# Scores transposed at the source, in 512-query groups with a per-key bias and the softmax sum from a matmul, for the 17 heads with the flattest ALiBi slopes

## What is computed

```python
xn = _layernorm(x, axis=-1)
q = (xn @ Wq).reshape(b, s, 32, 128)
k, v = (xn @ Wkv)[..., :128], (xn @ Wkv)[..., 128:]
scores = jnp.einsum('bqhd,bkd->bhqk', q, k) * scale
scores = jnp.where(causal, scores + slopes[h] * (pos_k - pos_q), -jnp.inf)
attn = jax.nn.softmax(scores, axis=-1)
x = x + jnp.einsum('bhqk,bkd->bqhd', attn, v).reshape(b, s, h) @ Wo + ffn(xn)
```

## Time and profile before

| | us |
|---|---|
| median of 2 runs, slowest core | 5608.9 (5591.86 and 5625.94) |
| the profiled execution, slowest core | 5518.5 |
| its span, first to last instruction | 5516.9 |
| spans of the 8 cores in it | 5493.5 to 5516.9 |
| mean granted TensorE clock of the cores | 0.765 to 0.768 of 2.4 GHz |

### The profile page before, as it was taken

The page is one execution under the profiler, slowest core; times in us unless marked ns, Lnnn a source line. Parts: engine busy times, 40 slices in busy tenths (PEclk is TensorE's granted clock), DMA queues, the critical chain, the costliest instruction groups (busy, mean ns, idle before and its releaser), DMA issues.

```text
span 5516.9 us, 49355 instructions; the slowest of 8 cores (5493.5 to 5516.9 us)
## 1 busy us (share of the span) xinstructions
PE 3486.3 (63%) x16923; PEld 1724.7 (31%) x17216; DVE 1495.5 (27%) x3505; ACT 1086.5 (20%) x1984; POOL 165.7 (3%) x171
## 2 busy tenths in 40 slices
PE   1575565656634499964766665665655444548999
PEld 1332222222222244432322232333333222224444
DVE  4212222222234300023122223333333444442000
ACT  4001111111133300012011222222222333331000
POOL 0000000000000000000000000000000000000000
PEclk9887777777755599976887777767767666668999
DMA  5342322232151157733422312112114000002764
GB/s 120 59 68 47 55 47 42 37 55 47 32 101 41 37 111 150 147 107 92 61 48 46 55 32 42 29 32 39 32 32 77 17 25 17 17 17 63 151 137 100
DMA packets 293247, 340.03 MB, mean 62 GB/s; under 512 B 28688, under 2 KB 249872, under 8 KB 282640
## 3 DMA queue, kind: packets, MB, share of 16 engines
q0 software_dynamic: 244480, 163.75, 22.1%
q1 hardware_dynamic: 30096, 139.54, 7.6%
q10 hardware_dynamic: 18432, 33.56, 1.6%
HBM read 467.01 MB, written 33.55 MB: 91 GB/s over the span
## 4 chain that ended last, share of the span: by engine, by line
PE 54%; DVE 15%; issue 13%; ACT 9%; DMA 8%; DVEq 1%; ACTq 0%; POOL 0%; SPq 0%; POOLq 0%
PE ps_a L424 19%; PE ps_a L686 16%; DVE scratch L603 8%; PE ps_c L557 7%; ACT astream L613 6%; DMA wstream<-wq 4%; PE ps_t L522 4%; PE ps_s L596 3%; DMA scratch<-x 2%; DVE scratch L531 2%; PE ps_a L691 2%; DVE cols L619 1%; ACT scratch L534 1%; DVE cols L196 1%; ACT astream L222 1%
## 5 line engine op out<-in xcount | busy, mean ns | idle before, releaser
L557 PE MATMUL ps_c<-scratch,vT 128*128 128x256 bf16 x1959 | 545.8, 381 | 1099.8 <-DVE scratch L531 554.1
L424 PE MATMUL ps_a<-xnT,wstream 128*128 128x512 bf16 x3975 | 1046.3, 425 | 122.6 <-DMA wstream<-wq 108.4
L613 ACT ACTIVATE astream<-scratch,cols 128x384 bf16<-128x384 f32 (+15 forms) x512 | 533.9, 1043 | 2208.0 <-DVE scratch L603 2206.9
L686 PE MATMUL ps_a<-xnT,QC 128*128 128x512 bf16 x4014 | 901.3, 380 | 6.3 <-ACT QC L565 2.1
L603 DVE TENSOR_TENSOR scratch<-ps_s,scratch 128x512 f32<-128x512 f32 (+3 forms) x1088 | 608.8, 592 | 254.5 <-PE ps_s L596 146.2
L424 PEld LDWEIGHTS ps_a<-xnT,wstream 128*128 128x128 bf16 x4096 | 443.8, 109 | 704.1 <-issue 335.3
L596 PE MATMUL ps_s<-kT,QC 128*128 128x512 bf16 (+3 forms) x1026 | 379.7, 422 | 447.9 <-DVE scratch L603 439.7
L557 PEld LDWEIGHTS ps_c<-scratch,vT 128*128 128x128 bf16 x1959 | 168.0, 115 | 1277.1 <-issue 1263.0
L686 PEld LDWEIGHTS ps_a<-xnT,QC 128*128 128x128 bf16 x4096 | 401.1, 98 | 486.2 <-issue 4.4
L522 PE MATMUL ps_t<-identsb,astream 128*128 128x128 bf16 x3593 | 495.3, 292 | 2.7 <-issue 2.7
L522 PEld LDWEIGHTS ps_t<-identsb,astream 128*128 128x128 bf16 x3593 | 403.1, 137 | 98.9 <-issue 28.3
(11 more groups left out here) (62 smaller groups left out, 1138.1 us busy)
## 6 DMA issues: line engine op xcount, KB each, us to landing
scratch<-ab SPq DMA_DIRECT2D x65, 1088.0 KB, 5.0
wstream<-wq POOLq DMA_DIRECT2D x64, 1024.0 KB, 13.9
xnT<-wo POOLq DMA_DIRECT2D x64, 1024.0 KB, 27.7
scratch<-x SPq DMA_DIRECT2D x16, 2048.0 KB, 8.2
scratch<-x SPq DMA_DIRECT2D x128, 256.0 KB, 4.9
out<-scratch ACTq DMA_DIRECT2D x128, 256.0 KB, 5.0
astream<-awt POOLq DMA_DIRECT2D x16, 1024.0 KB, 10.7
wstream<-bwt POOLq DMA_DIRECT2D x16, 512.0 KB, 37.2
```

Source lines behind the costliest of these rows:

```text
L424: E.matmul(ps_a[b][:], wq_half_view[hh][:, kk % 16, mm * 128:(mm + 1) * 128], xnT[:, kk, t2 * 512:(t2 + 1) * 512], start=(kk == 0), stop=( ...
L557: E.matmul(ps_c[b][:, 0:256], vT[:, jj * 128:(jj + 1) * 128], u[:, c0:c0 + 256], start=st, stop=fin), inc="pe")
L613: E.activation(uv[:, 0:LL], vv[:, 0:LL], AF.Exp, bias=c_negB, accum_out=c_Z[ss]), inc="ac")
L686: p.op("tensor", lambda E, b=bank, kk=k, pp=par, tt=t: E.matmul(ps_a[b][:], QC[:, kk, tt * 128:(tt + 1) * 128], wo_view[pp][:, kk, :], sta ...
```

## The change

From head 15 on, in both chunks, attention is computed in another form; heads 0 to 14 and all other stages are untouched.

- Scores come out transposed: one matmul gives 128 keys (on the partitions) by 512 queries (L539 of the changed kernel). The two groups `g2` of a head hold 512 queries each; group `g2` of chunk `c` has 8c + 4 g2 + 4 key blocks: 4 and 8 in chunk 0, 12 and 16 in chunk 1.
- The bias is slope times key position, relative to the last query of the group, less 30: one number per key, given to the exp as its per-partition bias (L558, table `bc`). The query part of the bias cancels in the softmax. Only the last four key blocks of a group cross the diagonal; VectorE adds a mask to them, in place in `ps_s` (L549, table `trx`).
- The exp result already has keys on the partitions, so it goes straight into the value matmul, 512 queries wide (L569). There is no transpose, no copy of one and no scaling of the row.
- The softmax sum comes from a second matmul with a column of ones, 1 x 512, into `ps_t` bank 0 (L574).
- At the end of a group VectorE copies that row (L585), takes its reciprocal (L589) and casts it to bf16 (L593), all on one partition; TensorE spreads it over 128 partitions by a matmul with a row of ones (L597); VectorE copies that (L602) and multiplies it into the result, writing `QC` (L609).
- `qpop(1)` stands once in each head, after group 0, so the 15 projection groups left are issued one in each of heads 15 to 29.
- The `ab` tables of heads 16 to 31 are not loaded any more (33 and 32 loads of 1088 KB in the two chunks become 16 and 16). At head 15 of each chunk the pending `emit_tv` is done, and GpSimd loads `trx` and `bc`, 128 x 896 and 128 x 576 fp32, for which VectorE and ScalarE wait.

```diff
+            if h >= 15:
+                if not sB_loaded:
+                    sB_loaded = True
+                    while tv_pend:
+                        emit_tv(tv_pend.pop(0))
+                    p.need("gpsimd", ("spb", 0))
+                    p.need("gpsimd", ("spb", 1))
+                    g_trx = p.op("gpsimd", lambda E: E.dma_start(out=v_trx, in_=dtrx),
+                                 inc="dgp", incby=16)
+                    g_bc = p.op("gpsimd", lambda E: E.dma_start(
+                        out=v_bc, in_=dbc), inc="dgp", incby=16)
+                    p.wait("vector", "dgp", p.cur("dgp"))
+                    p.wait("scalar", "dgp", p.cur("dgp"))
...
+                for g2 in range(2):
...
+                    for j in list(range(jlo, jhi)) + [None]:
+                        if j is not None:
+                            bank = scnt % 2
+                            scnt += 1
+                            p.need("tensor", ("ps_s", bank))
+                            pe_sc = p.op("tensor", lambda E, b=bank, hh=h, jj_=j,
+                                         qq=qt0: E.matmul(
+                                ps_s[b][:, 0:512], kT[:, jj_ * 128:(jj_ + 1) * 128],
+                                QC[:, hh, qq * 128:qq * 128 + 512],
+                                start=True, stop=True), inc="pe")
...
+                            if jj >= 0:
+                                off = 384 - 128 * jj
+                                p.wait("vector", "pe", pe_sc)
+                                gate_val = p.op("vector", lambda E, b=bank, oo=off:
+                                                E.tensor_tensor(
+                                    ps_s[b][:, 0:512], ps_s[b][:, 0:512],
+                                    v_trx[:, oo:oo + 512], ALU.add), inc="dv")
+                                gate_sem = "dv"
...
+                            ac_exp = p.op("scalar", lambda E, b=bank, ss=sl, hh=h,
+                                          ii=idx: E.activation(
+                                astream[:, ss * 1024:ss * 1024 + 512], ps_s[b][:, 0:512],
+                                AF.Exp, bias=v_bc[:, hh, ii:ii + 1]), inc="ac")
...
+                        if pend is not None:
+                            pj, psl, pac = pend
+                            p.wait("tensor", "ac", pac)
...
+                            pe_av = p.op("tensor", lambda E, b=avbank, jj_=pj, ss=psl,
+                                         st=first, fin=(pj == jhi - 1): E.matmul(
+                                ps_c[b][:, 0:512], vT[:, jj_ * 128:(jj_ + 1) * 128],
+                                astream[:, ss * 1024:ss * 1024 + 512],
+                                start=st, stop=fin), inc="pe")
+                            pe_z = p.op("tensor", lambda E, ss=psl, st=first,
+                                        fin=(pj == jhi - 1): E.matmul(
+                                ps_tf[0][0:1, 0:512], onescol[:],
+                                astream[:, ss * 1024:ss * 1024 + 512],
+                                start=st, stop=fin), inc="pe")
...
+                    dv_zr = p.op("vector", lambda E: E.tensor_copy(
+                        zr_f[:, 0:512], ps_tf[0][0:1, 0:512]), inc="dv")
...
+                    dv_rc = p.op("vector", lambda E: E.reciprocal(zr_f2[:, 0:512],
+                                                                  zr_f[:, 0:512]),
+                                 inc="dv")
...
+                    dv_rc = p.op("vector", lambda E: E.tensor_copy(zr_b, zr_f2[:, 0:512]),
+                                 inc="dv")
+                    p.wait("tensor", "dv", dv_rc)
+                    p.need("tensor", ("ps_t", 1))
+                    pe_bc = p.op("tensor", lambda E: E.matmul(
+                        ps_tf[1][:, 0:512], onesr[:], zr_b, start=True, stop=True),
+                        inc="pe")
...
+                    dv_zb = p.op("vector", lambda E: E.tensor_copy(zb_sb, ps_tf[1][:]),
+                                 inc="dv")
...
+                    dv_ctx = p.op("vector", lambda E, b=avbank, hh=h, gg=g2:
+                                  E.tensor_tensor(
+                        QC[:, hh, gg * 512:(gg + 1) * 512], ps_c[b][:, 0:512],
+                        zb_sb, ALU.mult), inc="dv")
...
+                    if g2 == 0:
+                        qpop(1)
+                continue
```

More of the change, by code:

```diff
@@ L94, in build_program @@
     dab = nc.dram_tensor("ab", [H, 128, S + 128], F32, kind="ExternalInput").ap()
+    dbc = nc.dram_tensor("bc", [128, H, 18], F32, kind="ExternalInput").ap()
+    dtrx = nc.dram_tensor("trx", [128, 896], F32, kind="ExternalInput").ap()
     dident = nc.dram_tensor("ident", [128, 128], F32, kind="ExternalInput").ap()
@@ L123, in build_program @@
     cols = sb("cols", [128, 48], F32)
+    onesr = sb("onesr", [1, 128], BF16)
+    onescol = sb("onescol", [128, 1], BF16)
     stats = sb("stats", [128, 8], F32)
@@ L151, in build_program @@
     ps_s = [psal("ps_s0", [128, 512], F32), psal("ps_s1", [128, 512], F32)]
-    ps_t = [psal("ps_t0", [128, 1024], BF16), psal("ps_t1", [128, 1024], BF16)]
+    ps_tf = [psal("ps_t0", [128, 512], F32), psal("ps_t1", [128, 512], F32)]
+    ps_t = [t[:].bitcast(BF16) for t in ps_tf]
     ps_c = [psal("ps_c0", [128, 512], F32), psal("ps_c1", [128, 512], F32)]
@@ L172, in build_program @@
     dv_eps = p.op("vector", lambda E: E.memset(c_negB, -40.0), inc="dv")
+    p.wait("vector", "dv", dv_eps)
+    dv_ones = p.op("vector", lambda E: E.memset(onesr[:], 1.0), inc="dv")
+    p.wait("vector", "dv", dv_ones)
+    dv_ones = p.op("vector", lambda E: E.memset(onescol[:], 1.0), inc="dv")
     ld_ident = p.op("gpsimd", lambda E: E.dma_start(out=ident[:], in_=dident),
@@ L741, in _host_constants @@
         _CACHED["ident"] = np.eye(128, dtype=np.float32)
+        x_ = np.arange(128, dtype=np.float32)
+        bc = np.empty((128, H, 18), dtype=np.float32)
+        for h in range(H):
+            for idx in range(18):
+                m = idx - 17
+                bc[:, h, idx] = SLOPES[h] * (x_ + 128.0 * m - 127.0) - 30.0
+        _CACHED["bc"] = bc
+        z_ = np.arange(896, dtype=np.float32)
+        _CACHED["trx"] = np.where(x_[:, None] > z_[None, :] - 384.0, NEG, 0.0
+                                  ).astype(np.float32)
     return _CACHED
@@ L756 @@
         "keyst": np.ascontiguousarray(np.asarray(L0_ffn_keys, dtype=np.float32).T),
-        "ab": cst["ab"], "ident": cst["ident"],
+        "ab": cst["ab"], "ident": cst["ident"], "bc": cst["bc"], "trx": cst["trx"],
     }
```

46 lines of the change are left out of this document (added).

## The result

| | before | changed |
|---|---|---|
| median over all runs, us | 5520.8 (10 runs) | 5263.1 (11 runs) |
| profiled execution, us | 5518.5 | 5200.0 |
| ratio | | 0.9442, 95% interval 0.9399 to 0.9485 |

The changed kernel is faster by 5.6%. The first two runs of the kernel before lie 1.4% and 2.0% above its fastest, while six of the later eight lie within 0.1% of it, so the 1.6% between them and the profile was no property of the kernel. The fair number to hold against the result is the forecast in the profile's own terms, 5091.5; measured were 5200.0. The gain was forecast at 427 us and is 318.

A forecast was written before the change was run, and what follows sets the result against it. Attention was taken as a chain of handovers with no full engine. Terms 35 + 707 + 456 + 210 + 102 = 1510 us against 1936.8 gave 5091.5 in profile terms, stated as 5180 in median terms, range 4980 to 5330.

The forecast's parts named there:

- What bounds attention: Attention before the change: no engine full, a chain of handovers with waits of 3.1 to 3.4 us ending on VectorE.
- The inner step: Key-block loop of heads 15 to 31: 0.88 us per plain step, 1.28 per masked, 707 us over 680 steps.
- The end of a group: 68 group ends where TensorE waits for VectorE's copy, reciprocal and cast: 2.9 us plus the reciprocal each, 456 us.
- R: Time of the 512-element reciprocal on one partition at a group's end: taken as 3.8 us, bounds 0.69 and 5.2.
- in the range: Chunk 0 ends before a masked block without projection between: delay up to 1.5 us, some 20 us, not in the sum.
- The Trainium skill on the reciprocal: Row reciprocal at group ends: if repeat count 8 means eight passes per element, 4.3 us, making that term 490 us.
- The clock: After each group-end standstill TensorE restarts at 1.2 GHz, slowing 3.5 steps by 0.4 us each: 102 us in all.
- Lead-in: Start of head 15: last old work and table loads, 15 us in chunk 0 and 20 in chunk 1; `wo` loads hidden.
- In terms of the median: Whole-kernel time: profile taken as 1.6% under the runs' median, so 5091.5 became about 5175, stated as 5180.
- the reciprocal as a fast pass: Rival at group ends: reciprocal takes 0.69 us, saving 211 us more, 4880 or about 4960 in median terms; chance 0.20.
- TensorE staying at 1.2 GHz: Rival for heads 15 to 31: steps of 1.28 us, saving only 132 us, 5387 or about 5475 in median terms; chance 0.06.
- The slower cases: Row reciprocal at L589 priced like 512 single ones: over 2% slower from 11.7 us, up to 10,500 us; chance 0.03.

The follow-up runs named there:

- a3_fill: Changed kernel plus 20 unread 512-column matmuls on TensorE between each group's last sum matmul and the spreading matmul; 5074.5 us, ratio 0.9209.
- a1_ones128: Changed kernel with 128 columns of ones instead of one as weights of the sum matmul; 5103.6 us, ratio 0.9261.
- a2_copy_for_recip: Changed kernel with a plain copy in place of the row reciprocal, result not normalised; 5007.3 us, ratio 0.9056.
- a4_qfirst: Changed kernel with each head's projection group issued ahead of group 0's spreading matmul instead of behind it; 5014.9 us, ratio 0.9091.

## Why the prediction came out as it did

Direction, mechanism and range held; the gain was a quarter smaller than forecast. Step by step, on core 4:

- **What bounds attention.** Right: a chain of handovers with no full engine, and still one after the change (a3_fill adds 1360 matmuls and gets faster).
- **The inner step, "value and sum 2 x 0.216".** This is the term that failed. It took the spacing of equal matmuls from the earlier trace rows for matmuls of unequal weights. Going to the one-column operand and back costs 0.09 us each way; the plain step was 0.954, not 0.88. It cost 93 us (a1_ones128), more than the whole 87 by which the stretches were longer than forecast; the other terms nearly cancel, which is luck. The exp was 0.69 rather than 0.72. Masked steps were 1.41, forecast 1.28; with equal shapes 1.31.
- **The end of a group.** Right in its structure, down to what TensorE waits for (a2_copy_for_recip, a4_qfirst). R was 3.34, forecast 3.8 within 0.69 to 5.2, 31 us less. The cast was 0.41 for 0.35, and the spreading matmul is followed after 0.51 us rather than 0.22: it runs at 1.2 GHz and changes the shape too, some 20 us in all. What was left "in the range" for chunk 0, a masked block behind VectorE's work, came: 1.6 us at each of 18 ends without projection (9.25 against 7.64 in chunk 1; 7.66 without masks).
- **Two slips of arithmetic.** The listed parts of an end add up to 2.92 us, and less the 0.16 they are 2.76, not 2.9; and 3.5 x 0.4 is 1.4, not 1.5. Put right, the sum would have been some 16 us lower and further from what was measured.
- **The Trainium skill on the reciprocal** (VectorE: DVE Perf Modes, section "Walkthrough: the 8-slice pipeline in each mode": an iterated divide with a repeat count of 8). Eight passes for each element would be 4.3 us, and the trace does not bear that out. From the 0.163 us for one element to the 3.34 for 512 are 6.2 ns for each further element, some six times the 1.05 of an ordinary pass. That it is several passes and not one agrees with an iterated divide.
- **The clock.** Forecast 102 us, measured at least 118 (a3_fill), but in other places: I charged only the steps, and half of it is in the projection groups, which start at 1.2 GHz right behind the standstill.
- **Lead-in.** 13.4 and 16.0 us from head 14's table to the first new exp, forecast 35 in all. The `wo` loads were not late: the output projection starts 0.51 us after the spreading matmul in both chunks.
- **In terms of the median.** The scaling by 1.016 rested on two runs of the kernel before; the median of all ten is 5520.8, at its profile. So it is luck that the stated 5180 lies within 0.4% of the 5200 measured: the wrong scaling made up for most of what the sum lacked.

The rivals: the reciprocal as a fast pass did not come, though the kernel with a copy in its place shows that its price was well sized (217 us of the stretches for the 211 given). TensorE staying at 1.2 GHz did not come; the clock rose in every group of chunk 1. The Trainium skill's warning there (TensorE: Matmul & The Clock Gate, section "A second HAM failure mode: psum-queue depth-cycling") describes what the ends of groups do, since the clock swings once for each; but the cause in this kernel is the standstill for the reciprocal, and with it filled the cycling through banks alone leaves the clock at 1.00 in chunk 1. The slower cases did not come.

Left open: most of the 12 us by which the untouched stages are longer on core 4 (before head 15 alone the cores of one run differ by up to 21 us), and why weights of another shape are not loaded beside the matmul in flight.

## What to carry to other kernels

A matmul with a few weight columns is not cheap because it is narrow: between wide ones it cost more than a wide one, and 128 columns of ones gave the sum already spread over all partitions, which made a second matmul, three copies and a wait unnecessary. Before a serial tail (copy, reciprocal, cast, matmul) is put at the end of a loop, look at what stands behind its last matmul in TensorE's list; here the tail made an end without a projection group 8.45 us long in front of the next group, and 1.98 us where its rebuilt form lies beside that group. And count a standstill of TensorE as long as these (4.9 us) twice, once for itself and once for the clock that it lets fall.

## What the runs showed of the hardware that I had not expected

- The spacing of 512-column matmuls at 2.4 GHz is 0.216 us for equal weight widths, and 0.306 to 0.322 into and out of weights of 1 or 32 columns between ones of 128; at 1.2 GHz 0.427 and 0.515 to 0.542. With equal widths the next weights are loaded from the start of the running matmul (0.002 us after it, a1_ones128); with unequal ones their load (0.08 to 0.10 us) starts 0.304 us or more after it.
- A reciprocal of 512 elements takes 3.34 us on one partition and 3.36 on 128 from PSUM.
- Twenty unread matmuls in each gap, 1360 in all, made the kernel 2.4% faster (5200.0 to 5074.5), by the clock alone.
